# Attention inner loop: both score halves issued ahead of both AV halves

## The reference

```python
# B, T, D = 2, 4096, 2048; 32 query heads, 8 key/value heads, head size 64; hidden 8192
xn = _layernorm(x, axis=-1)
x = x + attn(xn) + ffn(xn)
# attn: Q, K, V projections, rope on Q and K, K and V repeated 4 times
scores = jnp.einsum('bhqd,bhkd->bhqk', Q, K) / np.sqrt(HD)
w = jax.nn.softmax(scores, axis=-1)
attn = jnp.einsum('bhqk,bhkd->bhqd', w, V)
# out = attn @ Wo.T + bo
# ffn: silu(x @ w_gate.T) * (x @ w_up.T), then @ w_down.T
```

## Time and profile before

| what | us |
|---|---|
| timed, median of 2 runs | 4548.26 (4542.23 to 4554.29) |
| the profiled execution's own time | 4331.15 |
| its span on the slowest core (core 2) | 4329.6 |
| spans of the eight cores | 4317.5 to 4329.6 |
| PE busy in the span | 3278.8 |
| ACT busy in the span | 1274.6 |
| DVE busy in the span | 916.9 |

### The profile page before, as it was taken

How to read it: one execution, slowest core, us unless ns; L and a number is a source line. 1 busy time by engine, 2 the same in 40 slices (tenths; PEclk the granted TensorE clock), 3 DMA queues, 4 the chain that set the end, 5 groups by cost and what they waited for, 6 DMA issues and landing times.

```text
span 4329.6 us, 39154 instructions; the slowest of 8 cores (4317.5 to 4329.6 us)
## 1 busy us (share of the span) xinstructions
PE 3278.8 (76%) x14752; PEld 1207.5 (28%) x14922; DVE 916.9 (21%) x1025; ACT 1274.6 (29%) x1612; POOL 225.1 (5%) x428
## 2 busy tenths in 40 slices
PE   3655645555587888778888676799989959999888
PEld 0211211111122222222222221344434424444343
DVE  3233343333312111221111321210100021101000
ACT  1110011111166777667777665000000000000000
POOL 0000000000000000000000000011100001111000
PEclk9877866766688888878888777899999979999999
DMA  5242353433200000000000002799998868999887
GB/s 104 43 80 61 65 105 80 90 81 77 52 1 1 1 1 1 1 1 1 1 1 1 1 1 35 140 153 152 150 151 156 167 130 148 153 152 153 153 161 143
DMA packets 95350, 340.25 MB, mean 79 GB/s; under 512 B 10784, under 2 KB 10816, under 8 KB 90688
## 3 DMA queue, kind: packets, MB, share of 16 engines
q0 software_dynamic: 60608, 274.81, 38.8%
q1 hardware_dynamic: 34560, 62.93, 5.0%
HBM read 604.07 MB, written 8.39 MB: 141 GB/s over the span
## 4 chain that ended last, share of the span: by engine, by line
PE 44%; ACT 20%; DVE 15%; DMA 14%; issue 7%; DVEq 0%; POOL 0%; another core or an unknown queue 0%; ACTq 0%; SPq 0%; POOLq 0%
ACT ptab L461 18%; PE pb L608 10%; PE pb L598 9%; DMA wo_sb<-wo_t 7%; PE pb L304 6%; PE pb L645 6%; DMA xf_sb<-x_t 3%; PE pb L356 3%; DVE rz_sb L503 2%; DVE rz_sb L505 2%; PE pb L640 2%; DMA xf<-x_t 1%; DVE scrf L282 1%; DVE xt_sb L285 1%; ACT scrb L309 1%
## 5 line engine op out<-in xcount | busy, mean ns | idle before, releaser
L461 ACT ACTIVATE ptab<-pb,negb_sb 128x1024 bf16<-128x1024 f32 x1024 | 1037.9, 1227 | 410.1 <-PE pb L449 409.6
L598 PE MATMUL pb<-xt,wg_sb 128*128 128x512 bf16 x2008 | 471.0, 382 | 100.8 <-DVE xt L579 58.1
L474 PE MATMUL pb<-ptab,v_all 128*64 128x512 bf16 x1024 | 425.7, 416 | 67.2 <-DVE pb L433 62.5
L608 PE MATMUL pb<-xt,wu_sb 128*128 128x512 bf16 x2006 | 463.1, 381 | 2.6 <-DMA wu_sb<-wu_t 0.2
L645 PE MATMUL pb<-gated,wd_sb 128*128 128x512 bf16 x2009 | 445.2, 379 | 2.1
L449 PE MATMUL pb<-qt_all,kt_all 64*128 64x512 bf16 x2048 | 418.7, 401 | 17.0 <-ACT ptab L461 16.4
L479 PE MATMUL pb<-ptab,v_all 128*64 128x512 bf16 x1024 | 428.2, 418 | 0.0
L614 ACT ACTIVATE silu_sb<-pb 128x512 bf16<-128x512 f32 x128 | 76.4, 597 | 1183.9 <-PE pb L598 1183.9
L488 PE MATMUL pb<-ptab,ones_bf 128*1 128x512 bf16 x1024 | 397.3, 388 | 0.0
L484 PE MATMUL pb<-ptab,ones_bf 128*1 128x512 bf16 x1024 | 397.3, 388 | 0.0
L304 PE MATMUL pb<-xt_sb,wk_sb 128*128 128x512 bf16 x496 | 197.5, 528 | 209.1 <-DVE xt_sb L285 208.5
(11 more groups left out here) (100 smaller groups left out, 2132.4 us busy)
## 6 DMA issues: line engine op xcount, KB each, us to landing
wg_sb<-wg_t POOLq DMA_DIRECT2D x128, 512.0 KB, 6.6
wu_sb<-wu_t POOLq DMA_DIRECT2D x128, 512.0 KB, 6.6
wd_sb<-wd_t POOLq DMA_DIRECT2D x32, 2048.0 KB, 16.2
xf_sb<-x_t SPq DMA_DIRECT2D x128, 256.0 KB, 2.6
xt_sb<-x_t POOLq DMA_DIRECT2D x32, 512.0 KB, 13.4
wk_sb<-wk_t POOLq DMA_DIRECT2D x32, 512.0 KB, 5.4
wq_sb<-wq_t POOLq DMA_DIRECT2D x32, 512.0 KB, 5.1
wo_sb<-wo_t POOLq DMA_DIRECT2D x32, 512.0 KB, 19.5
```

Source lines behind the costliest of these rows:

```text
L461: exp_ab[(c, h)] = em.emit("scalar", (lambda par, h: lambda s: s.activation(ptab[:, 2048 * par + 1024 * h:2048 * par + 1024 * (h + 1)], ps ...
L474: em.emit("tensor", (lambda c, p, h, pt_a: lambda t: t.matmul(pava[0:64, 512 * h:512 * (h + 1)], v_all[:, VST * c + 65 * (2 * p):VST * c + ...
L598: mg = em.emit("tensor", (lambda par, dc: lambda t: t.matmul(pg[par][:, :], wg_sb[:, 2048 * par + 128 * dc:2048 * par + 128 * (dc + 1)], x ...
L608: mu_ = em.emit("tensor", (lambda par, dc: lambda t: t.matmul(pu[par][:, :], wu_sb[:, 2048 * par + 128 * dc:2048 * par + 128 * (dc + 1)], ...
```

## The change

Only the order of the calls in the chunk loop changes: S and EXP for both halves first, then AV for both halves of the chunk before. Every instruction, its operands and the events that it waits for stay.

```diff
         for c in range(NKCH):
-            for h in range(2):
-                S_half(c, h)
-                EXP(c, h)
-                if c >= 1:
-                    AV(c - 1, h)
+            S_half(c, 0)
+            EXP(c, 0)
+            S_half(c, 1)
+            EXP(c, 1)
+            if c >= 1:
+                AV(c - 1, 0)
+                AV(c - 1, 1)
         AV(NKCH - 1, 0)
         AV(NKCH - 1, 1)
```

## The result

The changed kernel is 1.0165 times as long as the one before, with a 95% interval of 1.0152 to 1.0178: 4410.63 us (median of 9 runs) against 4339.11 us (median of 8 runs), +72 us. That is slower by more than the measurement leaves open, and inside the 2% of "no change".

The account below looks back on a forecast made before the run. ACT was taken to bound the attention's steady part at 2.01 us per chunk; the new loop's 2.19 adds 81 us, less 6 at pair starts: +75 on the timed 4548 us gives 4623 us, 8-in-10 range 4560 to 4665.

Parts of the forecast that it names:

- the base: Whole kernel: the added 75 us was put on the timed runs' median of 4548.26 us, giving 4623 us, +1.6%.
- the 217 us: Whole kernel: timed runs' median exceeds the profiled execution by 217 us, which the trace does not explain; kept in the forecast.
- who sets the pace: Steady part of each pair: ACT is the bound at 1.005 us per half, PE has 0.25 us of room.
- the loop: Steady part, new order: two chunks take 1.63+0.49+1.11+1.005+0.14 = 4.375 us, 2.19 per chunk against 2.01.
- slots: PE's queue from S(c,1) to S(c+1,0): five slots of two matmuls side by side, 0.32+0.34+0.32+0.34+0.31 = 1.63 us.
- S to the start of the exponential: Steady part, PE to ACT: 0.49 us at full clock, a score matmul of 0.39 plus 0.10.
- hand-over to PE: Steady part: 0.14 us from the end of an exponential to the PE matmul that waits for it.
- 6 for the start: Start of each pair, at the low clock: gain of 0.4 us per pair, 6 us in all.
- Not slower: Steady part: the PE wait is hidden, ACT stays full, only the start's 6 us counts, 4542 us; chance 7%.
- Dearer hand-overs: Steady part: same mechanism but 2.24 us and more per chunk, +97 to +115 us, 4645 to 4663; chance 22%.
- The clock: Steady part: idle PE drops to 1.2 GHz, +524 us if it stayed there, a tenth if now and then; chance 8%.
- PE's slots longer in timed runs: Steady part: slots a fifth longer, before PE-bound at 2.33 us per chunk, after 2.39, +21 us, 4569; chance 11%.

Follow-up runs that it names:

- e1_one_group_between: Changed kernel with the first AV group, without its ones, moved between S(c,0) and S(c,1); 4329.6 and 4345.9 us.
- e3_fewer_ones: Changed kernel with the ones group of half h=1 left out and accumulators starting at 1; 4316 to 4323 us, ratio 0.9977 to the kernel before.
- e7_ones_twice: Changed kernel with the ones group of half h=0 issued twice; 4455 to 4502 us, ratio 1.036 to the kernel before.
- e2_start_only: Kernel before with only each pair's start in the changed order, halves taking turns from chunk 2 on; ratio 0.9994 to the kernel before.
- e4_short_exp_grouped: Changed kernel with exponentials of 512 instead of 1024 columns, the second head's left out; 4242 to 4256 us, ratio 0.9754 to the kernel before.

## Why the prediction was right or wrong

**Wrong: the base.** The step that failed is "the timed runs have a median of 4548.26, ... I add it as it is: 4623 us". The kernel's time is 4339 us, 8 us from the profiled execution's 4331, and the prediction had worked its sum out against that one: 4331+75 = 4406 us, +1.7%. Measured are 4410.6 us and +1.65%. The forecast was 212 us too high: the 217 us that I called unexplained and kept, less the 5 us by which 4406 was too low. The range of 4560 to 4665, built on the same base, misses for that reason only. The spans of all eight cores in the profile lay within 12 us at one clock, and two timed runs stood against them; with a gap of 5% between a profile and so few runs the range should have gone down to the profile's own time (on it, the same range is 4343 to 4448, and holds the result). The chances (slower by over 2%: 32%, within: 65%) hung on the ratio and stand.

**Right: who sets the pace, and the loop.** ACT was the bound of the steady part, with 0.25 us of room for PE. The loop was forecast at 4.375 us for two chunks and is 4.375 ((1348.85-1340.10)/2). Its terms: slots 1.63, measured 1.62 (ones to AV, the estimated one, 0.32, measured 0.31); S to the start of the exponential 0.49, measured 0.50; one exponential 1.11 and the next 1.005, measured 2.12 together; hand-over to PE 0.14, measured 0.14. That the total agrees to the last digit is luck: the errors of 0.01 us cancel.

The experiments change the work behind S(c,1). The steady part below runs from the end of EXP(3,1), a pair's eighth exponential, to the end of its last, over 16 pairs; the start runs from a pair's first exponential to the end of EXP(3,1). Both are read from all 1024 exponentials and are means of the eight cores of the profiled execution, in us. The sum is 224 loops (28 chunks, two to a loop, 16 pairs) of the work plus 0.50+2.115+0.14, and 4.5 us for a late exponential in each pair (last section); for the kernel before it is 896 exponentials of 1.005.

| kernel | work behind S(c,1) | loop | sum | steady part | start | whole attention |
|---|---|---|---|---|---|---|
| before | | | 900.5 | 900.6 | 226.8 | 1447.6 |
| e1_one_group_between | 1.28 | 4.035 | 908.3 | 909.0 | 219.4 | 1448.5 |
| e3_fewer_ones | 1.31 | 4.065 | 915.1 | 915.7 | 204.7 | 1435.8 |
| changed | 1.62 | 4.375 | 984.5 | 984.4 | 215.1 | 1519.7 |
| e7_ones_twice | 1.835 | 4.59 | 1032.7 | 1032.8 | 223.1 | 1579.1 |

One formula gives all four steady parts within 0.1%, and the start times are read to 0.01 us, which alone is worth 2 us over 224 loops. That is the mechanism, and it is shown: ACT's own 4.02 us for four exponentials is a floor, and whatever the loop has above it is paid in full, the 0.015 us of e1_one_group_between too.

**Size.** 28 chunks x 0.18 x 16 = 81 us less 6 for the start made 75; the attention grew by 72.1 on the mean of the cores. The table splits it. The steady part costs 83.8 us: 79.5 for the loop (81 in the sum, which rounded 0.1775 to 0.18) and 4.5 for the late exponentials, which the sum did not have. The starts give back 11.7 where 6 were forecast. The rest, round the tails, is 320.2 us in both. So the two sizes that were off, by 3 and by 6 us, partly cancel.

Why the start gave more: the sum took the stretch at the low clock as fixed, and it is not. Before, the clock rises 5.5 us after AV(0,0) on the mean of all pairs and cores; after, 4.6 us, and anywhere from 3.0 to 6.5 (3.3 to 5.8 before). In one pair it is early:

```profile
1610.66 0.61 PE L474 MATMUL pb<-ptab,v_all 128*64 128x512 bf16 x1 [3.14 <-DVE pb L433]
```

```profile
1613.54 4.16 ACT L461 ACTIVATE ptab<-pb,negb_sb 128x1024 bf16<-128x1024 f32 x4 [4.77 <-PE pb L449]
```

```profile
1610.66:1613.70 3.04, 3.04 (x12) 0.56 (x12) 0.00 (x0) 0.16 (x1) 0.00 (x0) 0.50 0.00 0
1613.80:1617.00 3.20, 2.87 (x20) 0.90 (x18) 0.00 (x0) 3.20 (x4) 0.00 (x0) 1.00 0.00 0
```

EXP(3,1) is the last of the four, and ends at 1613.54+4.16 = 1617.70, 7.0 us after AV(0,0). Before, in the pair of the rows, the third exponential from 1308.67 ended at 1311.79, 8.2 us after AV(0,0) at 1303.60. In the first pair looked at the gain is nothing, since the clock rises late there:

```profile
1320.92 0.60 PE L474 MATMUL pb<-ptab,v_all 128*64 128x512 bf16 x1 [3.14 <-DVE pb L433]
```

```profile
1326.97 4.13 ACT L461 ACTIVATE ptab<-pb,negb_sb 128x1024 bf16<-128x1024 f32 x4 [1.03 <-PE pb L449]
```

Here EXP(3,1) is the second in the row of ACT, two paces before its end: 1326.97+4.13-2.01 = 1329.09, again 8.2 us after AV(0,0), with the clock rising 6.1 us after it against 4.9 in the pair of the rows. Pairs of both kernels in which it rises after 4.5 to 5.0 us can be compared directly: EXP(3,1) ends after 7.73 us in the changed order and after 8.16 before, 0.43 us. So the forecast 0.4 us for the order is right, some 7 us in all by this estimate; the other 5 came with the clock and were not forecast. The same start in e2_start_only gains less, and there the clock rises after 5.7 us on the mean.

**The rivals.** Not slower, because adjacent groups spare PE time: PE is spared, 0.22 instead of 0.31 to 0.34 us, but only between the two S (seen in e4_short_exp_grouped, where nothing holds the second), and the loop needed five slots of 0.25. Dearer hand-overs: none was, to 0.01 us, but for one exponential in each pair. The clock: 1.00 through the steady part although PE waits there; no. PE's slots longer in timed runs: that may be so in the two runs that gave the 217 us, and no trace of them was kept; the runs that were compared do not have the 217 us.

**The gap between groups, and the length of an exponential.** The Trainium skill (TensorEngine Tiling (Array Packing), Key Properties) says that changing the tiling mode drains the engine. The runs agree as far as they go: S behind S 0.22 us (e4_short_exp_grouped), ones behind ones 0.21 (e7_ones_twice), any change between S, AV and ones 0.31 to 0.34. Whether the drain or the load of other weights makes the 0.1 us no run separates, since both repeated pairs also use the same weights. The Trainium skill (ScalarE: Activation LUTs, What ACT_TABLE_LOAD costs) prices an exponential at 1.133 us alone and 1.040 us in a row, and the estimate from it was a loop of 4.43 us; it is 4.375, with 1.11 and 1.005 us, so the rows were the better source here.

## What to carry to other kernels

When an in-order engine waits for the youngest result of another, count the work queued behind the wait: the loop is that work plus the hand-overs and the other engine's two instructions, and it may be longer than either engine's own work. Every microsecond of it above the slower engine's own work is paid. Spread the instructions that wait for a double buffer as evenly as the engine that frees it works, unless that engine is far from its bound; a grouping that spares PE time pays only where PE sets the pace. And work a percentage out against the execution that the trace shows, then ask whether the few timed runs are of the same kind before adding it to them.

## What the runs showed of the hardware that I had not expected

The exponentials fell into a pattern of period two: ACT is idle once for 0.25 us after four of them, not a little after each two, as the loop holds S(c,1) of one chunk and of the next but one. The prediction had allowed for it (S(c,0) every 2.0 and 2.4 us in turn) but not counted on it. Where the clock rises in a pair's start was fixed in the sum, and moves by over 3 us from pair to pair, as told above.

One exponential of each pair starts late without a cause in the rows. In the pair shown:

```profile
1370.73 4.13 ACT L461 ACTIVATE ptab<-pb,negb_sb 128x1024 bf16<-128x1024 f32 x4 [0.24 <-PE pb L449]
1375.38 3.12 ACT L461 ACTIVATE ptab<-pb,negb_sb 128x1024 bf16<-128x1024 f32 x3 [0.52 <-PE pb L449]
```

```profile
1374.61 0.78 PE L449 MATMUL pb<-qt_all,kt_all 64*128 64x512 bf16 x4
```

S starts at 1374.61, and the idle ACT 0.77 us later where it is 0.50 elsewhere; the idle time is 0.52 us instead of 0.24. It is EXP(25,0), and it is late by 0.27 to 0.30 us in all 16 pairs on all eight cores, in the changed kernel and in e1_one_group_between, e3_fewer_ones and e7_ones_twice alike: 16 x 0.28 = 4.5 us. So it is no accident of one execution; what holds it stays open. In the kernel before the same exponential is queued early enough to hide it: the steady part there is 896 exponentials of 1.005 us and nothing more. A queue with slack hides such a thing; a closed loop pays for it.
